# Two-layer gated cross-attention kernel: in the masked layer, the low parts of the odd feed-forward weight tiles move from VectorE to GpSimd

## The reference, cut to what matters

```
# layer 1 (the masked one), after its attention
h   = x_norm @ w1 + b1                  # (4096 x 512) @ (512 x 2048)
h   = float2fix(h, 8)                   # rounded to multiples of 1/256
h   = float2fix(pwlin_gelu(h), 8)       # interp between 33 points of the exact GELU
out = float2fix(h @ w2 + b2, 8)         # (4096 x 2048) @ (2048 x 512)
x   = x + tanh(g_ffn[1]) * out
```

## Time and profile before

| What | Value |
|---|---|
| median of 3 runs | 2407.02 us (2404.2 to 2410.87) |
| the profiled execution's own time | 2409.38 us |
| its span, first to last instruction | 2407.6 us |
| TensorE busy | 2352.2 us, 98% of the span |
| VectorE busy | 1504.9 us, 63% |
| ScalarE busy | 1181.1 us, 49% |
| GpSimd busy | 238.6 us, 10% |
| mean granted TensorE clock | 0.991 of full speed |

### The profile page before, as it was taken

One profiled execution on the slowest core, in us unless ns is written; L12 is line 12 of the kernel. 1 busy time (PEld: TensorE's weight loads), 2 busy tenths in 40 slices (PEclk: granted clock), 3 DMA queues, 4 the chain that ended last, 5 costly groups with the idle time before them and its releaser, 6 DMA issues.

```text
span 2407.6 us, 32695 instructions
## 1 busy us (share of the span) xinstructions
PE 2352.2 (98%) x12984; PEld 1793.4 (74%) x12984; DVE 1504.9 (63%) x2467; ACT 1181.1 (49%) x1912; POOL 238.6 (10%) x219
## 2 busy tenths in 40 slices
PE   7999999999999999999988999999999999999998
PEld 5566666688888888888765666666788888888886
DVE  5566666442222222223488888886988987988986
ACT  4554434442222222223335666666666666666665
POOL 1021112210000000000111111113000000000000
PEclk9999999999999999999998999999999999999999
DMA  3121112421101101102311111224301001110000
GB/s 130 36 88 53 53 54 80 161 80 53 50 4 53 53 1 53 53 3 86 121 64 50 67 68 67 67 71 145 105 29 43 36 36 36 36 38 33 36 35 19
DMA packets 89159, 140.95 MB, mean 59 GB/s; under 512 B 5040, under 2 KB 27952, under 8 KB 89008
## 3 DMA queue, kind: packets, MB, share of 16 engines
q1 hardware_dynamic: 89008, 138.87, 16.9%
HBM read 105.30 MB, written 33.55 MB: 58 GB/s over the span
## 4 chain that ended last, share of the span: by engine, by line
PE 39%; DVE 8%; ACT 2%; issue 2%; POOL 0%; DVEq 0%; ACTq 0%
PE l_lay_bank L69 19%; PE l_lay_score L69 11%; PE l_lay_score L1490 1%; PE l_lay_score L1546 1%; PE l_lay_score L1563 1%; DVE l_at_at_next L1089 1%; PE l_lay_score L1575 1%; PE l_lay_score L1567 1%; DVE l_at_h_lo L1103 1%; DVE l_at_at_next L1082 1%; PE l_lay_bank L1406 1%; DVE l_at_full L1078 1%; DVE l_at_full L1071 1%; DVE l_at_xTf_lo L975 1%; DVE l_at_maxes L1012 1%
## 5 line engine op out<-in xcount | busy, mean ns | idle before, releaser
L69 PE MATMUL l_lay_score<-l_at_tw_hi,l_at_h_hi 128*128 128x512 f32 x1024 | 401.5, 392 | 5.4 <-DVE l_at_h_lo L1103 4.8
L69 PE MATMUL l_lay_bank<-l_at_xTf_hi,l_at_tw_hi 128*128 128x512 f32 x1024 | 400.0, 391 | 0.0
L69 PE MATMUL l_lay_score<-l_at_tw_hi,l_at_h_lo 128*128 128x512 f32 x1024 | 398.8, 389 | 0.0
L69 PE MATMUL l_lay_bank<-l_at_xTf_hi,l_at_tw_lo 128*128 128x512 f32 x1024 | 398.4, 389 | 0.0
L69 PE MATMUL l_lay_bank<-l_at_xTf_lo,l_at_tw_hi 128*128 128x512 f32 x1024 | 398.4, 389 | 0.0
L69 PE MATMUL l_lay_score<-l_at_tw_lo,l_at_h_hi 128*128 128x512 f32 x1024 | 398.4, 389 | 0.0
L1063 DVE TENSOR_TENSOR l_at_h_lo<-l_at_full,l_at_h_hi 128x512 fp32r<-128x512 f32 x128 | 93.4, 729 | 468.5 <-ACT l_at_h_hi L760 468.5
L755 ACT ACTIVATE l_at_full<-l_lay_bank,l_at_lay_b 128x512 f32<-128x512 f32 x128 | 88.5, 691 | 456.6 <-PE l_lay_bank L69 456.6
L69 PEld LDWEIGHTS l_lay_score<-l_at_tw_hi,l_at_h_hi 128*128 128x128 f32 x1024 | 192.2, 188 | 49.3 <-DVE l_at_h_lo L1103 10.4
L69 PEld LDWEIGHTS l_lay_score<-l_at_tw_hi,l_at_h_lo 128*128 128x128 f32 x1024 | 192.2, 188 | 40.3
L69 PEld LDWEIGHTS l_lay_bank<-l_at_xTf_hi,l_at_tw_hi 128*128 128x128 f32 x1024 | 192.3, 188 | 40.1 <-issue 0.7
(11 more groups left out here) (196 smaller groups left out, 4063.0 us busy)
## 6 DMA issues: line engine op xcount, KB each, us to landing
both_x_in<-stream SPq DMA_DIRECT2D x25, 1024.0 KB, 5.6
l_at_xg<-stream SPq DMA_DIRECT2D x23, 1024.0 KB, 5.5
stream<-l_at_xg SPq DMA_DIRECT2D x22, 1024.0 KB, 4.3
l_at_tw_raw<-in_l_w SPq DMA_DIRECT2D x64, 256.0 KB, 5.5
both_x_in<-in_x SPq DMA_DIRECT2D x9, 1024.0 KB, 7.8
l_at_xg<-in_x SPq DMA_DIRECT2D x7, 1024.0 KB, 5.5
out<-l_at_xg SPq DMA_DIRECT2D x7, 1024.0 KB, 4.3
l_at_maskT_in<-in_maskT SPq DMA_DIRECT2D x16, 256.0 KB, 3.5
```

The lines of the kernel that those rows point to most:

```text
L69: done = nc.tensor.matmul(out, lhs[a], rhs[b], start=first and n == 0, stop=last and n == len(passes) - 1)
```

## The change

In the masked layer, GpSimd makes the low parts of tiles 3, 5, 7, 9, 11, 13 and 15 with the function that it has for tiles 0 and 1. Five of them stand before `x_rstd_of(NCH + 1)` in its order, two behind. VectorE keeps the even tiles. TensorE's waits count accordingly: `w_lo` for an odd tile, `w_lo_late` for an even one. Layer 0 stays as it is.

```
+        POOL_TILES = tuple(range(3, MT, 2))
+        low_on_pool = lambda m: m < 2 or (norm and m in POOL_TILES)
...
             widen(last, range(KT))
+            if norm:
+                for m in POOL_TILES[:5]:
+                    weights_lo(m)
             x_rstd_of(NCH + 1)
+            if norm:
+                for m in POOL_TILES[5:]:
+                    weights_lo(m)
...
             for q in range(QT):
-                weights_lo_late(2 + q)
+                if not low_on_pool(2 + q):
+                    weights_lo_late(2 + q)
                 y_back(last, q)
...
-                if f == 0 and m + 4 < MT:
+                if f == 0 and m + 4 < MT and not low_on_pool(m + 4):
                     weights_lo_late(m + 4)
...
                     if m < 2:
                         pe.wait_ge(w_lo, 2 * m + 2)
+                    elif low_on_pool(m):
+                        pe.wait_ge(w_lo, m + 3)
                     else:
-                        pe.wait_ge(w_lo_late, 2 * m - 2)
+                        pe.wait_ge(w_lo_late, m if norm else 2 * m - 2)
```

## The result

The changed kernel takes 2418.04 us (median of 7 runs, 2410.12 to 2420.96); the kernel before, timed with it, 2406.74 (7 runs, 2404.20 to 2410.87). The ratio is 1.0038 with a 95% interval of 1.0027 to 1.005, that is about 9 us slower (6.5 to 12.0 by the interval; the two medians are 11.3 us apart). The forecast was 2416.5 with a range of 2409 to 2420.

A forecast was written before the change was run, and what follows sets the result against it. TensorE bounds the kernel, with VectorE becoming the bound in the changed chunk. Stalls of 12.85 us, 13.55 with restarts, less 3.6 before, give +9.95, taken as +9.5: 2407.02 to 2416.5 us, range 2409 to 2420.

The forecast's parts named there:

- What bounds it: Whole kernel: TensorE, busy 98% of the span, is the bound; only its gaps count, 3.6 us in the chunk.
- Removed work is worth little: Masked layer's first feed-forward chunk: 8.4 us less VectorE work shortens pairs of turns by only 0.2 us each.
- The added work shuts VectorE out by 1.10 us for each instruction: Same chunk: each GpSimd instruction delays VectorE's two-SBUF-input work by 1.10 us, making odd turns 6.18 instead of 3.99.
- near 1.7: Expected profile sign: GpSimd's subtractions (L551) average above 1.29 us, near 1.7 in the masked layer's first feed-forward chunk.
- The walk: Tile-by-tile tally of TensorE's stalls in the chunk: 12.85 us, 13.55 with seven restarts, less 3.6 before: net +9.95.
- second product 8: First feed-forward chunk: TensorE due at 1742.7, low part ready at 1744.2, a stall of 1.5 us.
- second product 9: First feed-forward chunk: TensorE due at 1749.6, low part ready at 1751.2, a stall of 1.6 us.
- gaps at the turn of the chunk: Where the first feed-forward chunk ends: gives and takes a few tenths of a us; total taken as +9.5.
- both tile parts come when VectorE is in L1103 and behind: Odd turns: ScalarE's high parts are done some 0.9 and 1.45 us after the turn's start; hence 1.10 for each.
- A: Rival: in the chunk the engines hardly meet; 1.8 us won, 2405.2 us; chance 0.10.
- B: Rival: half the blocking, 1.1 us for a tile instead of 2.2; +4.2 us, 2411; chance 0.23.
- C: Rival: VectorE's lag lasts through the turn of the chunk; +13 to +18 us, 2420 to 2425; chance 0.07.

The follow-up runs named there:

- e1_none: Changed kernel without GpSimd's 14 instructions for odd tiles' low parts; TensorE reads the high part instead: 2406.72 us, ratio 0.9989 to the kernel before.
- e2_read: Kernel before, VectorE's work untouched, plus 14 GpSimd subtractions reading SBUF at the change's places, results unused: 2417.57 us, ratio 1.0031 to the kernel before.
- e3_write: Kernel before plus, at each of the change's 14 places, two GpSimd memsets that write SBUF and read nothing: 2411.10 us, ratio 1.0001.
- e6_tile7: Kernel before with the change made for tile 7 alone: 2409.76 us, ratio 1.0004 to the kernel before.

## Why the forecast was right, and where it was not

**What bounds it**: right. Behind the chunk no wait is new; TensorE is busy there for 88.91 of 89 us, where it was 88.30.

**Removed work is worth little**: right, and shown by e1_none: 8.4 us taken from VectorE give 2.3 (forecast 1.8). The idle 0.88 in even turns came as forecast.

**The added work shuts VectorE out by 1.10 us for each instruction**: right to 0.02 (1.79 less 0.69), turns of 6.18 as forecast. That the two engines exclude each other is shown by e2_read; that GpSimd's writing alone doesn't do it, by e3_write. GpSimd's own instructions grew to 1.56 on average, not to the "near 1.7" of the forecast's signs.

**The walk**: right in the sum, and in part by luck. Time lost by TensorE from start to start (the wait, without the slow restart):

| Place | forecast | measured |
|---|---|---|
| y_back (tile 3) | 0.65 | 0.6 |
| second product 2 | 2.8 | 2.5 |
| second product 4 | 1.4 | 1.3 |
| second product 6 | 3.2 | 3.1 |
| second product 8 | 1.5 | 0 |
| second product 9 | 1.6 | 2.7 |
| second product 10 | 1.7 | 0 |
| lower clock behind products 6 and 9 | 0 | 2.9 |
| gaps at the turn of the chunk | "a few tenths" | -1.0 |

The first four terms stand. From there a term is missing: the prediction reads the granted clock as 1.00 before and has no term for its fall, neither in the walk nor in a rival. Behind the gaps of 2.95 and 2.56 us the granted clock fell to the lower level (1.2 GHz). Six and then five matmuls followed one another at 0.427 us instead of 0.227, with a slower step at either end: 1.5 and 1.4 us more than an ordinary restart. TensorE was so late by itself that second product 8 found its input ready (due at 1741.52, L1111 ended at 1741.24); at the full clock it would have been due 1.5 earlier and, by my estimate from these rows, would have waited 1.3, near the 1.5 of the walk. So the term that was missing took the place of one that was there, and the sum hardly shows it. Second product 9 was worse than forecast. The step that failed is "both tile parts come when VectorE is in L1103 and behind": for tile 15 they came during the normalisation. VectorE's timeline there, then GpSimd's:

```profile
1745.10 2.87 DVE L951 TENSOR_SCALAR both_x_in<-both_x_in,l_at_lay_mv,l_at_lay_rstd 128x512 f32<-128x512 f32 x4
1747.89 0.74 DVE L1079 TENSOR_SCALAR l_at_full<-l_lay_bank,l_at_lay_b 128x512 f32<-128x512 f32 x1
1748.55 1.08 DVE L1111 SCALAR_TENSOR_TENSOR l_at_h_lo<-l_at_at_grid,l_at_h_hi 128x512 fp32r<-128x512 f32 x1
```

```profile
1746.09 3.00 POOL L553 TENSOR_TENSOR l_at_tw_lo<-l_at_tw_raw,l_at_tw_hi 128x512 fp32r<-128x512 f32 x2 [9.16 <-ACT l_at_tw_hi L756]
```

They cost the normalisation 0.96 (2.87 for 1.91) and L1111 0.40, and left the turn for tile 11 at 4.39 instead of 6.18, so that second product 10 had nothing to wait for. Last, of the gaps that the kernel before has where the chunk turns, the first (0.7) is gone and the second falls from 0.5 to 0.25, since TensorE is later there by itself. The sum of the right column, with five restarts of 0.1, less what was lost before (3.6) is 9.0, and the ruler shows 9.0. Of these, 2.9 are steps at the lower clock.

**Rivals.** A is what e1_none built: without the meeting the gain is 2.3 us, where 1.8 was priced. B was wrong: the instructions meet fully. C was wrong in its reason: the turn of the chunk gave 1.0 back. The clock stands in none of the three. The gaps of before, up to 1.49 us, showed no fall; longer gaps were a case that those rows could not speak for.

## What to carry to other kernels

Before elementwise work goes to an idle GpSimd, look at what VectorE does at the moments when the data is ready: instructions with two SBUF inputs are each held up by nearly the GpSimd instruction's own length, here 1.1 us to save 0.6. So is the normalisation, with one (2.87 for 1.91). Such work belongs where VectorE reads one operand from PSUM (L1079 beside a running L553 took 0.74, as ever) or waits, as for tile 5 here, or stays where it is. And the gain of relieving a busy engine is what its longest turns cost the bounding engine, not the time removed: 8.4 us removed gave 2.3. Last, when the walk leaves gaps of 2 us or more, price the restart too: it was 2.9 of 9.0 us here, and 4.7 of 8.1 in e2_read.

## What the runs showed of the hardware

**The clock after a gap.** TensorE's clock fell in the records of the changed kernel (granted 0.77 and 0.73 in the 5 us stretches above) behind waits of 2.95 and 2.56 us, and not behind one of 2.37; in e6_tile7 it fell behind one of 2.38. In e2_read it fell behind all three, of 2.08, 3.28 and 1.76. The first matmul of a slow row took 0.79 or 0.69 where it begins slow, and in e2_read's second and third gap the first one still took 0.50 and the slow ones came two to four matmuls later. So near 2 us a gap may or may not cost more; where it did, it was 1.4 to 1.6 us each time. No experiment kept the gaps and held the clock, so what a gap must be like for the clock to fall stays open.

**The scatter of the runs goes with the clock.** Of 27 runs of the kernel before, beside the first experiments, the 11 with a mean granted clock of 0.989 took 2410.84 to 2411.76 us, the four with 0.992 or more 2401.70 to 2406.24. Of the changed kernel's seven, the one with 0.993 took 2410.12 and the three with 0.987 or 0.988 took 2418.78 to 2420.96. Whether the falls behind its gaps are why its runs scatter more (10.8 us against 6.7) was not tested.

**GpSimd's memsets slow one kind of VectorE instruction and not another.** The normalisation (one tensor from SBUF, written to SBUF) was slowed by GpSimd's memsets, 2.52 against 1.91, while two-input instructions beside them were not, 0.68.
